# The experts' first layer as three rounded products in place of one full-precision product

## The reference

```python
x = _ln(hidden_after_attn, ln2_weight, ln2_bias).reshape(-1, H)      # 4096 tokens x 128
probs = jax.nn.softmax(x @ router_weight, axis=-1)                   # 8 experts
top_p, top_i = jax.lax.top_k(probs, 2)
...
cap = int(np.ceil(N * TOP_K / N_EXP * CAP_F))                        # 1280 rows for each expert
exp_in = padded_tokens.reshape(N_EXP, cap, H)
act = jax.nn.gelu(jnp.einsum('ech,ehf->ecf', exp_in, moe_w1), approximate=False)   # f = 512
exp_out = jnp.einsum('ecf,efh->ech', act, moe_w2).reshape(N_EXP * cap, H)
weighted = exp_out * padded_probs[:, None]
moe = jnp.zeros((N, H)).at[padded_ids].add(weighted)
return hidden_after_attn + moe.reshape(S, B, H)
```

## Time and profile before

| | |
|---|---|
| runs before | 1931.51, 1934.94, 1942.27 us; median 1934.94 |
| profiled execution | 1936.78 us, its span 1935.0 us |
| busy share of the span | PE 89%, PEld 68%, DVE 71%, ACT 61%, POOL 54% |
| granted clock of TensorE, mean | 0.945 of full speed |

### The profile page before, as it was taken

One profiled execution on the slowest core, in us unless ns is written; L12 is line 12 of the kernel. 1 busy time (PEld: TensorE's weight loads), 2 busy tenths in 40 slices (PEclk: granted clock), 3 DMA queues, 4 the chain that ended last, 5 costly groups with the idle time before them and its releaser, 6 DMA issues. The chain is left out here.

```text
span 1935.0 us, 43749 instructions
## 1 busy us (share of the span) xinstructions
PE 1719.2 (89%) x15588; PEld 1311.0 (68%) x15588; DVE 1374.0 (71%) x4606; ACT 1189.5 (61%) x2858; POOL 1041.2 (54%) x1590
## 2 busy tenths in 40 slices
PE   7999999999889999999999999999879998489930
PEld 5666666667667777777777777776656667379930
DVE  6688888873667788888888888897658876611127
ACT  3566666653588887778787787776415776234412
POOL 3466666763155665566666665566431442175375
PEclk9799999989999999999999999999999999589975
DMA  2000000000300000000000000000000000345322
GB/s 56 9 13 15 16 12 13 15 8 10 91 1 2 1 1 7 8 7 8 7 8 7 2 8 7 6 4 6 7 27 15 27 21 16 98 70 75 60 64 83
DMA packets 57823, 44.02 MB, mean 23 GB/s; under 512 B 13952, under 2 KB 50186, under 8 KB 57482
## 3 DMA queue, kind: packets, MB, share of 16 engines
q1 hardware_dynamic: 52330, 30.11, 5.4%
q0 software_dynamic: 4608, 9.45, 3.4%
q10 hardware_dynamic: 672, 1.67, 0.3%
HBM read 26.52 MB, written 13.63 MB: 21 GB/s over the span
## 5 line engine op out<-in xcount | busy, mean ns | idle before, releaser
L2279 POOL TENSOR_SCALAR probs<-probs,rsums 128x128 f32<-128x128 f32 (+1 forms) x512 | 210.0, 430 | 304.4 <-DVE rsums L2176 303.5
L1059 POOL TENSOR_SCALAR at_least<-magnitudes,candidates 128x512 bf16<-128x512 f32 x128 | 198.7, 1568 | 154.3 <-DVE candidates L948 154.3
L2160 DVE CUSTOM_DVE_ANT_0 probs<-dist,pq,nmin 128x128 f32<-128x128 f32 (+1 forms) x512 | 181.2, 409 | 74.5 <-PE pq L1620 74.2
L1900 ACT ACTIVATE probs<-probs,low 128x130 f32<-128x130 f32 (+1 forms) x512 | 227.7, 461 | 6.3 <-DVE low L2160 6.2
L1019 DVE TENSOR_REDUCE negmax<-ps_scores 128x4 f32<-128x1024 f32 x128 | 156.2, 1220 | 54.7 <-PE ps_scores L629 53.0
L810 ACT ACTIVATE pT<-ps_scoresT 128x1024 f32<-128x1024 f32 x128 | 131.2, 1025 | 54.8 <-PE ps_scoresT L638 47.1
L2170 DVE COPY pT<-pq 128x384 f32<-128x384 f32 x256 | 129.8, 547 | 4.3 <-PE pq L1635 4.3
L1813 ACT ACTIVATE qn<-pq 128x512 f32<-128x512 f32 x128 | 77.1, 602 | 81.2 <-PE pq L1477 79.6
L1620 PE MATMUL pq<-k1T,q1T 64*128 64x128 f32 (+1 forms) x1024 | 119.3, 351 | 0.6 <-ACT k1T L1828 0.5
L3297 POOL DMA_INDIRECT m_x<-token_rows,m_idx_put x80 | 75.9, 949 | 79.8 <-DVE m_idx_put L3227 33.3
L3249 DVE COPY m_y<-pm 128x256 f32<-128x256 f32 x40 | 17.0, 425 | 139.8 <-PE pm L3135 139.8
(11 more groups left out here) (541 smaller groups left out, 5283.6 us busy)
## 6 DMA issues: line engine op xcount, KB each, us to landing
expert_answers<-m_y SPq DMA_DIRECT2D x40, 128.0 KB, 2.0
m_w<-in_L_ffn_moe_w_dram SPq DMA_DIRECT2D x16, 256.0 KB, 5.9
x<-in_x_dram SPq DMA_DIRECT2D x16, 128.0 KB, 2.2
x_mid<-x SPq DMA_DIRECT2D x16, 128.0 KB, 1.9
y<-x_mid SPq DMA_DIRECT2D x16, 128.0 KB, 2.4
x_mid<-y SPq DMA_DIRECT2D x16, 128.0 KB, 1.8
cx<-x_mid SPq DMA_DIRECT2D x8, 256.0 KB, 2.9
token_rows<-c_hn SPq DMA_DIRECT2D x8, 256.0 KB, 2.0
```

Of the source, the lines that this page charges most:

```text
L1059: pool.tensor_scalar(at_least[:, a, :], mags[:, 512 * (a // 2):512 * (a // 2) + 512], cf[:, a:a + 1], None, ALU.is_ge).then_inc(mask_ready ...
L1900: ins = act.activation(probs[:, a, keys_nulls(i, w)], probs[:, a, keys_nulls(i, w)], ACT.Exp, bias=low[:, a, i:i + 1], scale=-1.0, accum_o ...
L2160: ins = dve.tensor_tensor_reduce(probs[:, a + t, keys(i, w)], dist[:, (1 - t) * P:N], ps[:, t * P:t * P + w], slopes[h], nmin[u][:, t, h:h ...
L2279: ins = pool.tensor_scalar(probs[:, a + t, keys(i, w)], probs[:, a + t, keys(i, w)], rsums[:, a + t, i:i + 1], 1.0, ALU.mult, ALU.mult)
```

## The change

Four kinds of tiles are added: hT_hi and hT_lo (two buffers each) and w1_hi and w1_lo (all experts), all of type F32R. ScalarE writes the rounded part as a copy, VectorE the rest as a difference. Layer one becomes three products for each 128 hidden features, summed in PSUM: w1_hi with hT_hi, w1_lo with hT_hi, w1_hi with hT_lo. The product of the two rests is left out. The rounding of hT stands in ScalarE's rows(n), behind the write of hT; the rest of item n+1 stands in VectorE's loop ahead of the copy of item n. The weights of two experts are prepared ahead of the loop, those of the others at two fixed items of each five.

```diff
         hT = sets(2, "m_hT", [P, W])
+        hT_hi = Sets([sb(f"m_hT_hi{i}", [P, W], F32R) for i in range(2)])
+        hT_lo = Sets([sb(f"m_hT_lo{i}", [P, W], F32R) for i in range(2)])
+        w1_hi = sb("m_w1_hi", [P, NE, F], F32R)
+        w1_lo = sb("m_w1_lo", [P, NE, F], F32R)
...
             def up(n):
                 if n % PER == 0:
                     pe.wait_ge(w_loaded[n // PER], 32)
-                ring.wait_read(pe, "hT", n)
+                    pe.wait_ge(*w_hi.at(n // PER + 1))
+                if n % PER == 0:
+                    pe.wait_ge(*w_lo.at(n // PER + 1))
+                pe.wait_ge(*h_hi.at(n + 1))
+                pe.wait_ge(*h_lo.at(n + 1))
                 for half in range(2):
                     ps = ring.open(pe, "up", n, half)
                     for i in range(2):
-                        c = 2 * half + i
-                        mm = pe.matmul(ps[:, i * W:(i + 1) * W], w1[:, n // PER, c * P:(c + 1) * P], hT[n][:],
-                                       start=True, stop=True)
+                        c = slice((2 * half + i) * P, (2 * half + i + 1) * P)
+                        o = ps[:, i * W:(i + 1) * W]
+                        pe.matmul(o, w1_hi[:, n // PER, c], hT_hi[n][:], start=True, stop=False)
+                        pe.matmul(o, w1_lo[:, n // PER, c], hT_hi[n][:], start=False, stop=False)
+                        mm = pe.matmul(o, w1_hi[:, n // PER, c], hT_lo[n][:], start=False, stop=True)
                     mm.then_inc(ring.filled("up", n, half), 1)
...
@@ ScalarE, rows(n)
+                if n >= 2:
+                    act.wait_ge(*h_lo.at(n - 1))
                 act.activation(hT[n][:], ps[:, 0:W], ACT.Identity, scale=ln2[:, 0:1], bias=ln2[:, 1:2])\
                     .then_inc(ring.read("hT", n), 1)
-
+                ring.wait_read(act, "hT", n)
+                act.activation(hT_hi[n][:], hT[n][:], ACT.Copy).then_inc(h_hi.sem, 1)
+
+            def round_w(e):
+                act.wait_ge(w_loaded[e], 32)
+                act.activation(w1_hi[:, e, :], w1[:, e, :], ACT.Copy).then_inc(w_hi.sem, 1)
+
+            for e in range(2):
+                round_w(e)
             rows(0)
...
@@ ScalarE, end of the loop over n
+                if n % PER == 1 and n // PER + 2 < NE:
+                    round_w(n // PER + 2)
...
@@ VectorE
+            def rest(n):
+                dve.wait_ge(*h_hi.at(n + 1))
+                dve.tensor_tensor(hT_lo[n][:], hT[n][:], hT_hi[n][:].bitcast(F32), ALU.subtract).then_inc(h_lo.sem, 1)
+
+            def weights_rest(e):
+                dve.wait_ge(*w_hi.at(e + 1))
+                dve.tensor_tensor(w1_lo[:, e, :], w1[:, e, :], w1_hi[:, e, :].bitcast(F32), ALU.subtract).then_inc(w_lo.sem, 1)
+
+            for e in range(2):
+                weights_rest(e)
+            rest(0)
             for n in range(ITEMS):
+                if n + 1 < ITEMS:
+                    rest(n + 1)
+                if n % PER == 2 and n // PER + 2 < NE:
+                    weights_rest(n // PER + 2)
                 if n >= YS:
                     dve.wait_ge(stored[n % YS], 16 * (n // YS))
                 ps = ring.wait(dve, "down", n)
```

More of the change, by code:

```diff
@@ L3079, in moe @@
         w_loaded = [sem(f"m_w{e}_loaded") for e in range(NE)]
+        h_ready = Counted(sem("m_h_ready"))
+        h_hi = Counted(sem("m_h_rounded"))
+        h_lo = Counted(sem("m_h_rest"))
+        w_hi = Counted(sem("m_w1_rounded"))
+        w_lo = Counted(sem("m_w1_rest"))
         x_loaded = [sem(f"m_x{i}_loaded") for i in range(XS)]
```

## The result

The changed kernel takes 1976.3 us (median of 4 runs, 1965.46 to 1985.16), against 1937.63 us for the kernel before (4 runs, 1931.51 to 1942.27: the three named above and a fourth of 1940.32). The medians are 38.7 us apart. The forecast was 1967, and 32 us slower.

A forecast was written before the change was run, and what follows sets the result against it. The last stage's chain through TensorE up to item 34 was taken as the bound; 31.3 us for 34 longer items plus 1 for the first items, 32 us on the median of 1934.94, gave 1967 us, range 1956 to 1977.

The forecast's parts named there:

- The bound: Last stage: the chain runs through TensorE to item 34, so item changes count until there; the last five are free.
- The products: Layer one on TensorE: twelve rounded products at 0.12 us, 1.44 us an item in place of 1.73, 0.29 shorter.
- The wait: Before layer one: TensorE waits for VectorE's copy, then hT_lo; 1.42 us from the transposes' start in place of 0.21.
- What was to cost nothing: ScalarE's rounding of hT and both engines' preparation of the weights: hidden behind other waits, no cost.
- The item: One item of the expert loop: 1.42 + 1.44 + 1.79 = 4.65 us, 0.92 more than 3.73; bounds 4.37 to 4.83.
- +1 for the first items: Start of the expert loop: the clock may rise one or two items later; +1 us, between -0.5 and +3.
- the case's own end: Upper end of the main forecast: 1935 + 37 + 3 = 1975 us; the forecast held 78%.
- (a): VectorE's rest blocked by POOL's gather issues: 6 us in all, 1973; up to 1993 if in step; 8%.
- (e): Layer one's rounded products no faster at all, 0.144 us each: 10 us more, 1977; 2%.
- (b): TensorE's clock falls from idling in the expert loop: for a third of the items, 2000 us; 4%.
- (c): Layer one's weight loads not hidden: 0.22 us a product, 1.2 us an item, 41 us, 2008; 3%.
- (d): The rest tile is ready when the transposes end, so layer one alone decides: 10 us faster, 1925; 3%.

The follow-up runs named there:

- The last run: Changed kernel with the rest issued ahead of the copy up to item 35 and behind it for items 36 to 39; 1931.54 us, ratio 0.9944 to the kernel before.

## Why the prediction was right

**The bound.** The chain of the earlier trace rows held: the loop counts from item 0 to item 34, the last five items run beside the lower gathers. The last run shows it. The lower gathers began 38.6 us later than before (1880.17 against 1841.58), 32.3 when both are counted from the first gather of x; 31 to 33 was the sign named.

**The products.** The forecast took 0.12 us between the bounds 0.110 and 0.131. In the item above, 1762.16 - 1760.98 = 1.18 us for ten steps, 0.118 each: twelve are 1.42, against 1.44. The row of 512 columns was the right neighbour: its half is 0.115. The shares of 24-row products were 7% under and 11% over. Layer one alone gained the forecast 0.29 us an item, as the run without the rest shows. The Trainium skill, FP8 and Floating Point Precision, section TensorE Precision Notes, counts four passes for a full product. A quarter of the full product measured here, 0.432 / 4, is 0.108, and a rounded product took 0.118, so three cost 0.82 of the full one and not 0.75.

**The wait.** From the start of the transposes to the copy 0.27, copy 0.42, to the rest 0.16, rest 0.42, and to the load 0.07. The trace has the first product's start 0.03 after the load, with 0.35 us in place of 0.28; counted back one step of 0.118 from the second product (1760.98) it is 1760.86, 0.11 after the load. So taken, the wait is 1.45 us, against 1.42. The sum of wait and products does not need that step: 1759.41 to 1762.28 is 2.87, against 2.86. The largest error is the rest, 0.42 in place of 0.40: its model L2068 reads one input from PSUM, this one reads both from SBUF, which may be the reason and was not tested. Each term came from one or two rows, and none is off by more than 0.02.

**What was to cost nothing.** ScalarE's rounding of hT was done 4.2 us ahead of its use. The weights' rounding took 0.62 us and their rest 0.68, and the items in which they stand are no longer than the others, but for one named in the next paragraph.

**The item.** 1.45 + 1.42 + 1.79 = 4.66, forecast 4.65. The mean over 34 items is 4.70, since the first item of each expert takes 4.82: there the load comes 0.23 us after the rest, not 0.07. The forecast's 0.05 for extra waits was the only allowance for such a thing, and too small, but it falls on 7 items only, 1.1 us. The first three items took 4.59. One item took 5.02; its copy started 0.36 us late. A rest of the weights stood ahead of that copy in VectorE's queue, but it had ended 3 us before, and the five other such copies are not late: what held this one is open.

**The sum.** 31.3 for the items was 32.9; +1 for the first items was -0.6, just outside its bounds. I had expected a later rise of the clock to cost more than the shorter layer of items 0 and 1 saves; it did not rise later. The microsecond from 11 to 12 after the first gather of x, in the kernel before and in the changed one (columns as above), has the same granted clock, and the one ahead of it 0.50, the one behind it 1.00 in both:

```profile
1707.22:1708.22 1.00, 1.00 (x5) 0.84 (x5) 0.00 (x0) 0.69 (x2) 0.70 (x2) 0.73 0.88 33
```

```profile
1713.46:1714.46 1.00, 1.00 (x8) 1.00 (x8) 0.00 (x0) 0.91 (x2) 0.69 (x2) 0.73 1.11 41
```

Behind copy 34 it was 0.6 less. Up to copy 34 the sum is 32.4 against 32. The median moved by 39, and the interval of the ratio, 29 to 44 us, holds both; the profiled execution's remaining 6 us lie ahead of the stage.

**What was luck.** The item was foreseen term by term. That the median, 1976.3, lies in the range of 1956 to 1977 is in part luck: it is 0.7 us under the upper end, two of the four runs lie above it, and the case's own end was 1975. The two that lead from there to 1977 are the rivals (a) and (e), which the traces refute. Of the 9.3 us between forecast and median, 2.7 are the fourth run of the kernel before; the rest is of the size by which the stages ahead differ from execution to execution.

**The rivals.** (a) *Gathers block VectorE:* refuted. The rest and those who wait for it, in the changed kernel (minimum, median, maximum in ns):

```profile
L3274 DVE TENSOR_TENSOR m_hT_lo<-m_hT,m_hT_hi x40: 424/424/426, 1708.3 to 1891.6; 128x256 fp32r<-128x256 f32 x40
```

None of 40 is longer than 426 ns, though in the item above GpSimd is issuing a gather from 1760.07 to 1761.01 right across it; in the run with the rest ahead the longest of the 40 took 449 ns. The Trainium skill, SBUF — State Buffer, section Who interferes with whom, says that such a VectorE instruction contends with a GpSimd instruction that reads SBUF, but also that a probe saw `tensor_tensor` stall no DMA whose descriptors GpSimd makes. This trace agrees with the second for the issue of gathers. (b) *The clock falls:* refuted, 1.00 over the whole loop with TensorE busy 78% of it. With the rest twice it was busy for still less, and the clock stayed (stretch of that run, columns as above):

```profile
1750.00:1800.00 50.00, 35.83 (x294) 33.73 (x293) 13.04 (x32) 21.95 (x42) 19.36 (x20) 1.00 0.33 53
```

(c) *Weight loads show:* refuted; the products follow each other in 0.118 us with a load for each. (d) *The stall is covered:* this was the way the change could have won, and it does as soon as the queue's order lets it. (e) *Products no faster:* refuted by the 0.29 us.

## What to carry to other kernels

Before a producer is put into a queue, read what stands ahead of it there, and what that waits for: a short instruction behind a wait for the consumer's own last work makes two engines take turns, even if all its inputs are early. Such a wait is the sum of the rows along the loop (0.27 + 0.42 + 0.16 + 0.42 + 0.07 + 0.11 here, the last counted as said), and can be worked out from instructions of the same size elsewhere in the trace. Where the consumer runs one step ahead of what the queue waits for, issue its producer one step earlier: here one changed index, with rest(1) ahead of the loop, turned 1.9% slower into 0.7% faster. Two buffers were still enough, since ScalarE writes hT_hi of item n+2 only when layer one of item n is done.

## What was not expected of the hardware

The first item of an expert loads its weights later than the others. One of them, with the rest that it waits for:

```profile
1755.44 0.42 DVE L3274 TENSOR_TENSOR m_hT_lo<-m_hT,m_hT_hi 128x256 fp32r<-128x256 f32 x1
...
1756.08 0.19 PEld L3139 LDWEIGHTS pm<-m_hT_hi,m_w_hi 128*128 128x128 f32 x1 [1.35 <-issue]
1756.11 0.36 PE L3139 MATMUL pm<-m_hT_hi,m_w_hi 128*128 128x256 f32 x1 [1.14 <-DVE m_hT_lo L3274]
```

The load came 0.22 or 0.23 us after the rest in place of 0.07 or 0.08, seven times out of seven. Such an item has three more waits, long satisfied (w_loaded, w_hi, w_lo). That they are the cause is not shown, and two things speak against a plain cost of such waits: in the program they stand ahead of the wait for the rest, where TensorE is idle anyway, and with the rest ahead of the copy the same three add nothing at six of the seven items (3.43 or 3.44 us like the others, and 3.51 once).

The three-product form pays because a rounded product of 256 columns with a weight load of its own takes 0.118 us, where a full-precision one takes 0.43 (two steps of 0.216): 0.35 for three.

The same kernel's stages ahead of the experts took 1689.9 to 1707.3 us in the profiled executions, with one program text for all of them. A change of 10 us can be read from the items of one trace, but from times only over many runs.
